# Row blocks of every fourth row, X loaded ahead of the matrix chunks, and column sums reordered by products, in a two-layer graph kernel on one Trainium2 core

## What is computed

```python
# layer 0: rows 0 to 2047 are users, the others items
u = par_u[0] * par_u[1] * (diag_u[:, None] * x_u @ W_u) + x_u      # the same for the items
h = adj @ (adj.T @ e)                                               # e = u and i one above the other
x = layernorm(x + layernorm(h) * gamma + beta + x)
# layer 1
deg  = adj.sum(axis=0) + 1.0
dinv = rsqrt(deg)
z    = dinv[:, None] * (x @ W)
out  = relu(dinv[:, None] * (adj.T @ z + z) + b)
x    = layernorm(x + out)
```

## Time and profile before

| | us |
|---|---|
| median of three runs | 645.34 |
| the profiled execution, its own time | 644.01 |
| its span, first to last instruction | 642.3 |
| PE busy | 605.3 |
| DVE busy | 317.0 |
| ACT busy | 138.9 |
| POOL busy | 106.7 |

### The profile page before, as it was taken

One profiled execution on the slowest core, in us unless ns is written; L12 is line 12 of the kernel. 1 busy time (PEld: TensorE's weight loads), 2 busy tenths in 40 slices (PEclk: granted clock), 3 DMA queues, 4 the chain that ended last, 5 costly groups with the idle time before them and its releaser, 6 DMA issues.

```text
span 642.3 us, 15855 instructions
## 1 busy us (share of the span) xinstructions
PE 605.3 (94%) x7310; PEld 292.2 (46%) x7310; DVE 317.0 (49%) x347; ACT 138.9 (22%) x208; POOL 106.7 (17%) x126
## 2 busy tenths in 40 slices
PE   6899999999999999999999998999999999978774
PEld 4435545554554555455554566554443434313112
DVE  2577877757576876747586673212040402203004
ACT  2003260603305060421506054111000101001001
POOL 3055250401305050220505031100000000000000
PEclk9999999999999999999999999899999999999998
DMA  8998869595977959596895807999999999999992
GB/s 231 374 368 320 310 225 366 183 367 184 380 272 280 358 178 367 188 362 241 282 364 178 295 3 274 391 403 392 402 410 413 409 413 409 411 412 410 413 398 79
DMA packets 93221, 204.10 MB, mean 318 GB/s; under 512 B 14780, under 2 KB 14820, under 8 KB 93156
## 3 DMA queue, kind: packets, MB, share of 16 engines
q1 hardware_dynamic: 87556, 201.72, 84.1%
q10 hardware_dynamic: 5600, 1.38, 1.0%
HBM read 201.78 MB, written 1.31 MB: 316 GB/s over the span
## 4 chain that ended last, share of the span: by engine, by line
PE 80%; DMA 13%; DVE 3%; SPq 2%; ACT 1%; issue 1%; ACTq 0%
PE psum L755 34%; PE psum L852 22%; PE psum L940 12%; DMA slot<-in_adj_dram 6%; PE psum L860 5%; DMA cut_last<-in_adj_dram 3%; DMA cut<-in_adj_dram 3%; PE psum L796 2%; DVE cut L597 1%; DMA X<-in_x_dram 1%; PE psum L960 1%; PE psum L809 1%; PE psum L922 1%; PE psum L910 1%; SPq L253 1%; SPq L256 1%
## 5 line engine op out<-in xcount | busy, mean ns | idle before, releaser
L597 DVE STREAM_TRANSPOSE cut<-slot 128x2048 f32<-128x2048 f32 x80 | 177.8, 2280 | 62.6 <-PE psum L852 62.3
L755 PE MATMUL psum<-slot,E 128*64 128x512 f32 x888 | 201.7, 596 | 1.2 <-DMA slot<-in_adj_dram 0.8
L852 PE MATMUL psum<-cut,T 32*64 32x256 f32 x5120 | 147.9, 377 | 1.4 <-DVE cut L597 1.2
L852 PEld LDWEIGHTS psum<-cut,T 32*64 32x64 f32 x5120 | 115.1, 131 | 47.5 <-issue 30.2
L372 POOL COPY turned<-cut_last 32x1024 f32<-32x1024 f32 x80 | 82.7, 1034 | 252.7 <-PE psum L860 241.5
L755 PEld LDWEIGHTS psum<-slot,E 128*64 128x64 f32 x888 | 60.9, 137 | 123.2 <-issue 115.5
L415 ACT ACTIVATE turned<-cut_last 32x1024 f32<-32x1024 f32 x80 | 84.4, 1055 | 17.0 <-DVE cut_last L597 10.2
L406 ACT ACTIVATE T<-T 32x256 f32<-32x256 f32 x60 | 24.8, 414 | 239.1 <-DVE T L575 237.9
L698 DVE TENSOR_TENSOR T<-psum,dinv 128x256 f32<-128x256 f32 x10 | 4.2, 425 | 144.6 <-PE psum L960 144.2
L940 PE MATMUL psum<-slot,E 128*64 128x512 f32 x272 | 64.6, 596 | 6.2 <-DMA slot<-in_adj_dram 6.2
L940 PE MATMUL psum<-cut,E 128*64 128x512 f32 x224 | 53.4, 597 | 4.0 <-DMA cut<-in_adj_dram 4.0
(11 more groups left out here) (111 smaller groups left out, 295.5 us busy)
## 6 DMA issues: line engine op xcount, KB each, us to landing
slot<-in_adj_dram SPq DMA_DIRECT2D x136, 1024.0 KB, 8.7
cut<-in_adj_dram SPq DMA_DIRECT2D x35, 1024.0 KB, 17.3
cut_last<-in_adj_dram SPq DMA_DIRECT2D x10, 1024.0 KB, 13.5
turned<-in_adj_dram SPq DMA_DIRECT2D x10, 1024.0 KB, 17.5
X<-in_x_dram SPq DMA_DIRECT2D x5, 256.0 KB, 8.7
out_dram<-T ACTq DMA_DIRECT2D x10, 128.0 KB, 9.9
T<-in_L_gnn_W_u_dram ACTq DMA_DIRECT2D x2, 16.0 KB, 2.9
T<-in_L_gnn_W_i_dram ACTq DMA_DIRECT2D x2, 16.0 KB, 3.1
```

Of the source, the lines that this page charges most:

```text
L597: v.transpose(to.rearrange("p c (j k r) -> p j k c r", j=JB, r=Q32), slot[c % NS][:, :, :].rearrange("p k (j c r) -> p j k c r", j=JB, r=Q ...
L755: return mm(acc[half[b % 2], :], E[:, b, :], view[:, b % CB, :], start=(b < 2), stop=(b >= NB - 2))
L852: last = mm(acc[half[h], a, u * 2 * P:(u + 1) * 2 * P], T[step % 2][rows_a, jb, (c - a) % 4, :], cut[u][rows_a, c, h, :, jb * P:(jb + 1) * P],
```

## The change

**Rows.** A block of 512 rows is now dealt so that partition p holds rows 4p to 4p+3 of it; block b = 4q + k holds every fourth row of the 512. In all three row views (`x_rows`, `out_rows`, `adj_rows`) q comes first, then p, then k. So four rows of X or of the output are 1 KB that lie together in HBM, where there were four pieces of 256 B. Pieces of adj stay at 2 KB and 4 KB. Columns of adj keep their order.

**X.** All five groups of X are issued ahead of the first chunk. On SP's queue, behind group 0 of X (T, turn and par are where the diagonals and parameters go):

```diff
-    x_rows = x.rearrange("(b p) f -> p b f", p=P)
-    out_rows = out.rearrange("(b p) f -> p b f", p=P)
-    adj_rows = adj.rearrange("(b p) j -> p b j", p=P)
+    x_rows = x.rearrange("(q p k) f -> p q (k f)", p=P, k=CB)
+    out_rows = out.rearrange("(q p k) f -> p q (k f)", p=P, k=CB)
+    adj_rows = adj.rearrange("(q p k) j -> p q k j", p=P, k=CB)
...
-                sp.dma_start(view, adj_rows[:, q * CB:(q + 1) * CB, J * JW:(J + 1) * JW]).then_inc(landed, 16)
+                sp.dma_start(view, adj_rows[:, q, :, J * JW:(J + 1) * JW]).then_inc(landed, 16)
...
-            load_x(1)
+            for g in range(1, NG):
+                load_x(g)
             for c in range(NJ * NQ):
...
-                if c + 2 < NG:
-                    load_x(c + 2)
...
             for step in range(NJ):
                 spread_T(step)
-                if step == NJ - 1:
-                    act.wait_ge(dinv_sum, 1)
-                    nc.scalar.activation(dinv[:, :], dinv[:, :], ACT.Sqrt).then_inc(dinv_root, 1)
                 move(step)
+
+            act.wait_ge(dinv_sum, 1)
+            nc.scalar.activation(dinv[:, :], dinv[:, :], ACT.Sqrt).then_inc(dinv_root, 1)
...
-                act.dma_start(out_rows[:, J * JB:(J + 1) * JB, :], Y[1][:, par_ * JB:(par_ + 1) * JB, :])\
+                act.dma_start(out_rows[:, J, :], Y[1][:, par_ * JB:(par_ + 1) * JB, :].rearrange("p b f -> p (b f)"))\
                    .then_inc(out_stored[par_], 16)
...
             def sum_degrees():
 
-                dve.wait_ge(t_ready, 2 * NJ)
-                late = RES * JB
-                link(v.tensor_scalar(mask[:, late:NB], deg[:, 0:NB - late], 1.0, None, ALU.add))
-                link(v.tensor_scalar(mask[:, 0:late], deg[:, NB - late:NB], 1.0, None, ALU.add))
+                dve.wait_ge(deg_turned, 1)
+                link(v.tensor_scalar(by_row[1][:, :, RES:NQ], deg_turn[:, :, 0:NJ - RES], 1.0, None, ALU.add))
+                link(v.tensor_scalar(by_row[1][:, :, 0:RES], deg_turn[:, :, NJ - RES:NJ], 1.0, None, ALU.add))
...
-            nc.tensor.transpose(bank[5][:, 0:NB], diag, ident[0:NB, 0:NB]).then_inc(diagT_done, 1)
+            for k in range(CB):
+                last = nc.tensor.transpose(scale_turn[:, k, :], diag[:, k::CB], ident[0:NQ, 0:NQ])
+            last.then_inc(diagT_done, 1)
...
+            def turn_degrees():
+
+                pe.wait_ge(t_ready, 2 * NJ)
+                for jb in range(JB):
+                    for k in range(CB):
+                        last = mm(deg_turn[jb * Q32:(jb + 1) * Q32, k, :], ident[:, k::CB], deg[:, jb::JB],
+                                  start=True, stop=True)
+                last.then_inc(deg_turned, 1)
...
                     for i in range(UNITS * JB // T_ROUNDS):
                         last = h_group(step, u, jb + i)
+                    if final and n == 0:
+                        turn_degrees()
...
-                    last = mm(o_turn[J % RES][:, jb, :], turn[J % RES][:, jb * P:(jb + 1) * P], fold[:, :],
+                    last = mm(o_turn[J % RES][:, jb, :], turn[J % RES][:, jb::JB], fold[:, :],
```

More of the change, by code:

```diff
@@ L77, in build @@
         WM = before[:, 256:256 + 3 * P].rearrange("p (w n) -> p w n", n=P)
-        diag = before[0:NB, 640:640 + P]
         W_out = sb("W_out", [P, P])
@@ L88, in build @@
         C = sb("C", [P, GB, F])
+        diag = turn[0][0:NQ, :]
         xT = [turn[1][:, :], sb("xT", [P, JW])[:, :]]
@@ L109, in build @@
         mask = scale
+        by_row = [v[:, :].rearrange("p (q k) -> p k q", k=CB) for v in (scale, mask)]
         rsum = sb("rsum", [P, GB])
@@ L132, in build @@
         y_turn = bank[3]
+        scale_turn = bank[5][:, 0:NB].rearrange("p (k q) -> p k q", q=NQ)
+        deg_turn = bank[6][:, 512 - NB:512].rearrange("p (k q) -> p k q", q=NQ)
         yw = bank[2].rearrange("p (b f) -> p b f", f=F)
@@ L172, in build @@
         t_ready = sem("t_ready")
+        deg_turned = sem("deg_turned")
         spread_act = sem("spread_act")
@@ L252, in load @@
             def load(view, landed, q, J):
-                sp.dma_start(view, adj_rows[:, q * CB:(q + 1) * CB, J * JW:(J + 1) * JW]).then_inc(landed, 16)
+                sp.dma_start(view, adj_rows[:, q, :, J * JW:(J + 1) * JW]).then_inc(landed, 16)
             def load_x(g):
-                sp.dma_start(X[:, g * GB:(g + 1) * GB, :], x_rows[:, g * GB:(g + 1) * GB, :])\
-                  .then_inc(x_loaded[g], 16)
+                q = g * GB // CB
+                sp.dma_start(X[:, g * GB:(g + 1) * GB, :].rearrange("p (q k) f -> p q (k f)", k=CB),
+                             x_rows[:, q:q + GB // CB, :]).then_inc(x_loaded[g], 16)
             load_x(0)
-            sp.dma_start(diag[0:USERS, :], diag_u.rearrange("(b p) -> b p", p=P)).then_inc(scales_loaded, 16)
-            sp.dma_start(diag[USERS:NB, :], diag_i.rearrange("(b p) -> b p", p=P)).then_inc(scales_loaded, 16)
+            sp.dma_start(diag[0:USERS // CB, :], diag_u.rearrange("(q j) -> q j", j=JW)).then_inc(scales_loaded, 16)
+            sp.dma_start(diag[USERS // CB:NQ, :], diag_i.rearrange("(q j) -> q j", j=JW)).then_inc(scales_loaded, 16)
             sp.dma_start(par[:, 0:2], par_u.unsqueeze(0).to_broadcast([P, 2])).then_inc(scales_loaded, 16)
             sp.dma_start(par[:, 2:4], par_i.unsqueeze(0).to_broadcast([P, 2])).then_inc(scales_loaded, 16)
-            load_x(1)
+            for g in range(1, NG):
+                load_x(g)
             for c in range(NJ * NQ):
@@ L311, in _ @@
                     else:
-                        sp.dma_start(pair[m], adj_rows[:, m * WB:(m + 1) * WB, k * RES * JW:(k + 1) * RES * JW])\
+                        sp.dma_start(pair[m], adj_rows[:, m // 2, m % 2 * WB:(m % 2 + 1) * WB,
+                                                       k * RES * JW:(k + 1) * RES * JW])\
                           .then_inc(landed, 16)
@@ L549, in _ @@
             dve.wait_ge(diagT_done, 1)
-            link(v.tensor_scalar(scale[:, 0:USERS], bank[5][:, 0:USERS], par2[:, 0:1], None, ALU.mult))
-            link(v.tensor_scalar(scale[:, USERS:NB], bank[5][:, USERS:NB], par2[:, 1:2], None, ALU.mult))
+            users = USERS // CB
+            link(v.tensor_scalar(by_row[0][:, :, 0:users], scale_turn[:, :, 0:users], par2[:, 0:1], None, ALU.mult))
+            link(v.tensor_scalar(by_row[0][:, :, users:NQ], scale_turn[:, :, users:NQ], par2[:, 1:2], None, ALU.mult))
             for g in range(NG):
@@ L622, in _ @@
                 copy_t(step, step % 2)
+                for q in late_:
+                    cut_chunk(step * NQ + q)
                 if step == NJ - 1:
                     sum_degrees()
-                for q in late_:
-                    cut_chunk(step * NQ + q)
                 if 1 <= step <= NG:
```

## The result

| | before | with the change |
|---|---|---|
| median, us (six runs each) | 645.1 (642.85 to 647.1) | 650.63 (648.17 to 652.91) |
| profiled execution, us | 644.01 | 649.99 |
| its span, us | 642.3 | 648.0 |
| granted PE clock over the span | 0.991 | 0.975 |

The ratio is 1.0081, with an interval from 1.0052 to 1.0110: the change makes the kernel 0.8% slower. I go through the same views in the same order as before.

The account below looks back on a forecast made before the run. PE bounds the first pass, PE's path to the release at 443.86 and then DMA's speed set the end; start -1.9, degrees +0.8, stores -0.6, tail -0.1 sum to -1.8 us: median 643.5, range 639.8 to 648.0.

Parts of the forecast that it names:

- term on degrees: Last step of the first pass: 32 degree instructions ahead of unit 1 start it 0.8 us later (-0.5 to +2.0).
- three signs of being wrong: Speed after 460 us off over 1%, PE never waiting at chunk 12, or degree products outside 0.9 to 3.2 us.
- Start: Start of the first pass: X landing earlier lets PE begin chunk products sooner, -1.9 us (-0.9 to -3.0).
- Turns: Tail, last two strips: turns take weights 16 bytes apart, taken as 0, up to +1.7 us.
- Rival 2: Degree products and last two turns: weights 16 bytes apart load slower by factor f; 649.5 at f = 2; chance 0.14.
- Stores: Second pass: output stores in larger pieces leave more room beside the loads, -0.6 us (0 to -2.1).
- Rival 3: Loads of adj, mainly behind 446 us: new row order changes DMA's speed; 2% is 3.6 us either way; chance 0.16.
- rival 1: Start: chunk 12 comes 3 us earlier, so PE's chain binds and the start gives all, -3.5, 641.8 us; chance 0.24.
- rival 4: X's and the output's pieces are no cheaper, so only the order counts: -0.1, 645.2 us; chance 0.06.

Follow-up runs that it names:

- experiment 8: The change with 93 more tiny idle products at PE's start: 646.15 us against 644.62 for the kernel before, ratio 1.0042.
- experiment 9: The kernel before with only tiny idle products added at PE's start: 35 more 649.49 us, ratio 1.0087; 98 more 643.45 us, ratio 0.998.
- experiment 5: The kernel before with only X's five loads, still in 256-byte pieces, moved ahead of the chunks: 642.88 us against 642.74, ratio 1.000.
- experiment 11: Kernel before with X ahead and 98 tiny products: 642.89 us, ratio 0.999; the change with turns' loads together and 63 tiny products: 644.68 us, ratio 1.0011.
- experiment 3: The change with SP's first spare load held until the third quarter of the last step's products is done: 650.47 us, ratio 1.0117 to the kernel before.

## Why the prediction was wrong

**The step that failed** is the end of the term on degrees: unit 1 starts 0.8 later, "and it passes on in full to 443.86 and to the end". The size was fair: L814 took 1.40 us, between the bounds of 0.9 and 3.2 (2.0 was taken). What failed is that PE's row behind it was taken as rigid: counted in products and waits, and not in instructions that have to be fetched. Added instructions move the ends of the blocks. One came to lie inside unit 1, 6 us after SP's first spare load, PE lost 2.76 us there, and the half clock followed. From the last fold to the release PE's path grew by 7.0 us where the prediction had 0.8, so the release was 4.2 us later and not earlier. Experiments 8 and 9 show this cause from both sides. None of the three signs of being wrong that the prediction named came up (a speed after 460 us off by 1%, no wait at the thirteenth chunk, degree products outside 0.9 to 3.2 us): they watched its terms, and most of the loss lay in none of them.

By the figure of the Trainium skill (TensorE: Matmul & The Clock Gate, LDWEIGHTS) the 32 instructions would have taken an estimated 0.9 us; they took 1.40, 0.044 us each.

- **Start, -1.9 (from -0.9 to -3.0).** It was -2.8 in this profile, near the upper end. PE's first chunk product came at 18.7 and not at 20.3: the first projection ended at 12.23 (9.62 + 2.61) where the term had up to 13.2, and the three groups behind took 2.17 each and not 2.38. PE waited for chunks until 39.21 and 47.25, so the room of DMA did bind, as the term says. DMA gave back about what I had kept as the limit (336 to 388 GB/s from 10 to 20 us). But the size is partly luck: in the nine profiles of kernels with the new rows and X ahead, that fold comes from 2.8 us earlier to 1.4 later than before (median 1.1 earlier). And a gain before 372 us isn't one at the end: experiment 5 has 2.2 us of it and a ratio of 1.000.
- **Turns, 0 (up to +1.7).** Here the row that I said was missing decides: +2.0 in the two last strips (2 x 0.98). Rival 2 was right at this place with f about 2 (16 loads of 0.12 us more), and wrong at the degrees, where it started from 0.099 us an instruction and 0.044 was measured. Its 649.5 at f = 2 lies near the 650.6 measured, but that is luck: it needs 6.3 us of degree products, and they took 1.40. The Trainium skill (SBUF — State Buffer, section Door 1: The DMA port swizzle, the note on cachelines) says that an access that crosses into a new 16-byte line pays a penalty; the trace agrees at the turns (329 ns a load and not 192), and for the degree products there is no row without the step to compare. This is a term that was mis-sized, about a third of the loss in these two profiles.
- **Stores, -0.6.** The stores' queue moves 1760 packets and not 5600, and a store lands in 5.8 us (median of ten) and not in 9.9, but the loads show no clear gain: 410 and 411 GB/s from 508 to 524 and from 524 to 546 us, where the earlier trace rows have 408 and 412. In the tail, which grew by 1.6 where the turns grew by 2.0, a gain of 0.4 us is left for them and all else. No more can be told from the traces.
- **Rival 3, the row order and DMA's speed.** Refuted for the second pass: 411 and 409 GB/s, as before. For the first pass there is something in it, at 2 KB pieces, as experiment 11 says. The prediction did not look there because PE bounds that pass.
- **Rivals 1 and 4.** The start gave most of what rival 1 asks (-2.8 of -3.5), and X's pieces were cheaper, against rival 4. Neither was what set the end.

**What the loss is made of, in medians.** The change stands at 1.0081; without the broken unit at 1.0042 (experiment 8), so the pause and what follows it cost 0.4%, 2.5 us. With the turns mended as well it is 1.0001 and 1.0011: another 0.3 to 0.4%, 2 to 2.6 us, of which the turns' own rows show 2.0. In the other order the shares come out otherwise: mending the turns first gives 1.0065, 0.2%, and removing the pause then 0.5 to 0.6%. In the kernel before, the 35 idle products alone cost 0.9%. The intervals are 0.2 to 0.3% to each side, so these shares are rough: in one order the two parts are about equal, in the other the pause is the larger, and together they are the whole. In the marks of the profiled execution pause, degrees and clock weigh more, since the trace of before is one of that kernel's quick ones.

**Open.** Why PE's clock falls a second time isn't known; it does so between 436 and 450 us in 13 of the 16 profiles, with and without a pause. That PE's pause ends with the arrival of a block is shown by its place by count and by the packet that starts 2.3 to 2.6 us before PE goes on. That this packet waits behind the spare loads is inferred from two things, the absence of a pause when the loads come later, and the steady 8.0 to 9.1 us from the first load to the moment PE goes on; no row shows when the packet is asked for. No kernel here is clearly faster than before: the best two, at 0.998 and 0.999, have intervals that take in 1.

## What to carry over

Where a change adds or takes instructions on the engine that bounds a kernel, ask also what it does to where the blocks of its program end: if the trace shows a pause with "issue" as its cause shortly after a burst of DMA, add a few dozen empty instructions in idle time and see whether the pause moves, before explaining the difference by the change. Put a burst of loads so that no block's end falls into the microseconds behind it. Take strided accesses out of the matrix engine's weights and put them where a single copy reads PSUM: here that copy stayed at 0.61 us.

## What was new about the hardware

- **A pause of PE at a block's end behind a burst of loads.** PE goes on 8.0 to 9.1 us after SP issues the first of a row of 1 MB loads (eleven profiles with a pause, ten of them 8.5 or more), and the pause takes what is left of that time when PE gets there: 0.98 to 3.23 us. A 16 KB packet of the instruction queue starts 2.3 to 2.6 us before PE goes on, and such packets come about once for 128 matmuls (57 for 7345). Where that packet started before the first load (392.5 and 393.04, experiment 3), no pause is seen.
- **PE's clock behind the pause.** The mean granted clock from 396 to 406 us is 0.50 to 0.66 in the seven profiles with a pause of 2.3 us or more, 0.58 to 0.79 in the four with 1.0 to 1.3 us, and 0.83 to 1.00 in the five without one; the half clock is the 1.2 GHz level, and eight small products take 1.86 us at it for 1.05. So a longer pause goes with a longer half clock, but it isn't the only thing ahead of such a fall: the kernel of experiment 3 has 0.50 from 404 to 408 without a pause, after PE had waited between the small products.
- **Weights 16 bytes apart.** 128 columns of float32: a load reads 329 ns in the profile instead of 192, and a turn of eight takes 2.08 us instead of 1.10. ScalarE reading PSUM 16 bytes apart takes 0.61 us (128x512 float32), as without the step. ScalarE writing SBUF one number at a time with a step of 512 bytes takes 1.05 us.
- **Small pieces.** From 10 to 20 us X in 1 KB pieces, with the chunks behind it, goes with 388 GB/s, and in 256-byte pieces among the chunks with 336. With the 256-byte pieces ahead of the chunks (experiment 5) it is 236 GB/s from 6 to 10 us, while X alone loads, and 379 behind.
